# A graph attention and normalisation kernel: another order of work at the beginning, and the transpose of h moved into the step before

## The chip, the cores and the metric

The kernel runs on one core of a Trainium2 chip, with its five engines: TensorE (PE: matmuls and transposes), VectorE (DVE), ScalarE (ACT), GpSimd (POOL) and SyncE (SP, which issues every transfer here). The metric is the device time of one execution in microseconds; less is better. Inputs and outputs lie in the chip's main memory, and the clock runs from launch to the last store.

## The reference

There are 128 graphs of 64 nodes with 384 features, all in float32. Two graph layers stand between residual additions and normalisations:

```python
x = layernorm(x + L0(x, adj))            # eps 1e-5
x = layernorm(x + L1(x, adj))
# L0: masked attention, 12 heads of 32, per graph
q, k, v = x @ Wq + bq, x @ Wk + bk, x @ Wv + bv
s = where(adj > 0, q k^T / sqrt(32) + beta * adj, -9e15);  out = softmax(s) v
# L1: two layers, each with weights Wl, Ws, Wr of 384 x 384
a = softmax(h h^T / sqrt(384)) * adj;  attn = a / (sum(a) + 1e-10)
ctx = (attn above the diagonal) (h Wl^T + bl) + diag(attn) * (h Ws^T + bs) + (attn below it) (h Wr^T + br)
h = relu(layernorm(ctx, eps=1e-12) * g + b)
```

## The kernel before

**Units and stages.** A unit is 256 tokens: four graphs, held as T = 2 tiles of 128 tokens, each with two graphs. There are 32 units. The kernel is one software pipeline over steps s = -2 to 32. In step s four units are in work at once: `EARLY` (unit s+2: projections of q, k and v), `MID` (unit s+1: scores, softmax, attention output and the first residual normalisation, which leaves h0), `LATE` (unit s: the two layers of L1) and `FINAL` (unit s-1: the last normalisation and the store). Step -2 has only `EARLY` (called `begin` in the code), step -1 has `EARLY` and `MID` (`second`), step 0 is the first with `LATE`, step 30 has no `EARLY` any more and step 31 no `MID`.

**Split products.** Every float32 product with a weight is made of three matmuls: `product` (lines 304 to 306) multiplies hi by hi, hi by lo and lo by hi, where hi is the value in the rounded type fp32r and lo is the rest. So each weight (nine of them: V, Q, K and six of L1) is first split: ACT copies it to `w_hi` (L521 in three pieces for V, L529 for the others), DVE subtracts to get `w_lo` (L689, L695). x transposed (`xT_in`) is split in the same way by ACT (L536) and POOL (L990), and h transposed by ACT (`hT_hi`, L572) and DVE (`hT_lo`, L774). The raw weights land in three slots `w_raw` laid over the tile `late`, so a load of weight n >= 3 waits until the weight three before has been split.

**Order.** Nothing is scheduled by a tool: each engine has a function `step(st)` that issues its instructions in an order written by hand, and semaphores tie the engines together (`need` waits for a count that follows from the unit's number). Each engine works strictly in its own order. PE's order in a full step is:

- `transpose_h`: six 128x128 transposes of h0 (L398) into PSUM banks 4 and 5 (`HT_BANKS`);
- `scores` of `MID`: 96 small matmuls (L357) into banks 0 to 3;
- `gram(0)`: h times h transposed (L421, 24 matmuls) into bank 6, from `hT`, which ACT copies out of banks 4 and 5 (L570). It also waits until the sum of the unit before has left bank 6 (`ctx_ready`, DVE L837);
- `project_sides(0)`: four times nine matmuls with `hT_hi` and `hT_lo`, into banks 7, 4, 5 and 6; the first waits until the second half of the unit before has left bank 7 (`ctx_ready`, DVE L846);
- `transpose_e(0)` (L449), `project_self(0)` (twice nine matmuls), `mix(0)` (L467, 16 matmuls);
- `project_v`, `project_qk` parts 0 and 1, `transpose_z` (L408), `transpose_probs` (L372), `project_qk` part 2, `attend` (L387);
- `gram(1)`, `project_sides(1)`, `transpose_e(1)`, `project_self(1)`, `mix(1)` for the second layer.

The next step then begins with `transpose_h`. ACT in the end of a step normalises h0 (L617), scales the self term (L606, and in two halves L610), and in the next step splits x of `EARLY` (L536), then takes `hT` (L570) and `hT_hi` (L572).

**The beginning.** Step -2 loads x transposed, the weights V, Q, K and small columns in this order; PE then projects v of unit 0, then q and k of unit 0 in three parts m (18 matmuls each: nine for q, nine for k, 128 columns of the weight). V goes to banks 3 and 0, q and k to banks 1 and 2, where part 2 waits until part 1 has been read out (`QK_BANKS`). `take_qk` on ACT (L544, L546) moves them out. Step -1 has the scores of unit 0, v of unit 1 (which waits for `s_masked`, DVE L744, because its banks hold scores), the transposes of the probabilities, `attend`, and q and k of unit 1. V moves inside SBUF by four transfers (`v_halves`), issued by SP. The bias rows of L1 are one transfer of 1.5 MB (`vectors`).

Of the kernel before, what the change touches and what calls it, by code (L numbers as in the profile page):

```python
# [5 lines left out]
F32 = mybir.dt.float32  # L6
# [22 lines left out]
STAGES_BEFORE, STAGES_AFTER = 2, 1  # L29
NEG = 9000000000000000.0  # L30
# [60 lines left out]
def resnorm_kernel(nc, x, xT, adj, adjT, w, cols, beta, bv, vectors, out):  # L91
    ctx = ExitStack()
    with ctx:
# [39 lines left out]
        c = [c0, c1]  # L133
        RAW = 3
        w_raw = [late[:, r * KC * D:(r + 1) * KC * D].rearrange("p (k d) -> p k d", k=KC)
# [3 lines left out]
        columns = sb("columns", [P, 4, KC])  # L139
        bq_col, bk_col, g0_col, b0_col = (columns[:, i, :] for i in range(4))  # L140
        beta_col = sb("beta_col", [P, 1])
# [39 lines left out]
        wv_hi_set, wv_lo_set = sem("wv_hi_set"), sem("wv_lo_set")  # L181
        raw_in = [sem(f"raw_in{r}") for r in range(RAW)]
# [42 lines left out]

        block = ctx.enter_context(nc.Block())
# [3 lines left out]
        def _(sp):  # L230
# [5 lines left out]
            def load_x(st, ahead):  # L236
                slot = st.slot(ahead)
                need(sp, x_added, st.count(ahead - 2, 2, 2))
                sp.dma_start(x_in[:, slot], x[st.unit(ahead)]).then_inc(x_loaded[slot], 16)
                sp.dma_start(adj_in[:, slot], adj[st.unit(ahead)]).then_inc(adj_loaded[slot], 16)  # L240
                for g in range(GRAPHS):
                    half = slice(g * N, (g + 1) * N)
                    sp.dma_start(adjT_in[half, slot, :, half], adjT[st.unit(ahead), half]
                                 ).then_inc(adjT_loaded[slot], 16)

            def raw_weight(n):
                if n == RAW:
                    sp.wait_ge(wv_hi_set, KC)
                    sp.wait_ge(wv_lo_set, KC)
                if n > RAW:  # L250
                    sp.wait_ge(w_hi_set, n - RAW)
                    sp.wait_ge(w_lo_set, n - RAW)
# [4 lines left out]
            sp.dma_start(columns[:, :, :], cols).then_inc(cols_in, 16)  # L257
            sp.dma_start(beta_col[:, :], beta.partition_broadcast(P)).then_inc(cols_in, 16)
            raw_weight(1)
            raw_weight(2)  # L260
            sp.dma_start(bv_row, bv.partition_broadcast(P)).then_inc(bv_in, 16)
            sp.wait_ge(tiles_cleared, 4)

            def step(st):
                if st.unit(EARLY) == 0:
                    load_x(st, MID + 1)
                    for n in (3, 4, 5):
                        raw_weight(n)
                if st.unit(MID) == 0:
                    raw_weight(6)  # L270
                    raw_weight(7)
                if st.has(EARLY + 1):
                    load_xT(st, EARLY + 1)
                if st.has(MID + 1) and not st.unit(EARLY) == 0:
                    load_x(st, MID + 1)
                if st.unit(EARLY) == 0:
                    sp.dma_start(rows[:, 1:9, :].rearrange("p r d -> p (r d)"), vectors.partition_broadcast(P)
                                 ).then_inc(rows_in, 16)
                if st.unit(MID) == 0:
                    raw_weight(8)  # L280
# [3 lines left out]
                if st.has(EARLY):  # L284

                    need(sp, v_staged, st.count(EARLY, 2, 2))
                    need(sp, o_scaled, st.count(MID, 2, 2))
                    for g in range(GRAPHS):
                        for half in range(2):
                            src = v_stage[g * N:(g + 1) * N, :, half * PAIRS:(half + 1) * PAIRS, :]  # L290
# [798 lines left out]
```

## Time and profile before

| | before |
|---|---|
| median of 3 runs | 1321.81 us (1319.84 to 1321.83) |
| the profiled execution, its own time | 1321.77 us |
| span from first to last instruction | 1320.0 us |
| PE matmul busy | 1268.5 us (96%) |
| DVE busy | 997.4 us (76%) |
| ACT busy | 624.3 us (47%) |
| POOL busy | 369.0 us (28%) |
| chain that ended last | PE 95%, issue 1%, ACT 1%, DVE 1%, DMA 1% |

The profile is one execution. In its timeline a row is a start in us from the span's start, a duration, the engine, the line, what is written and read with the shapes, and a count; in square brackets stands the idle time of that engine before the row and the instruction whose end released it. Matmuls overlap, so the difference of two starts tells what a group costs PE, and a matmul's own duration does not. PEclk or "granted clock" is 1.00 where TensorE runs at 2.4 GHz and 0.50 at 1.2 GHz.

### The profile page before, as it was taken

The numbers are of one execution on the slowest core, as the hardware profiler recorded it, in microseconds if no ns is written. First come the engines' busy times: TensorE is split into PE (matmuls) and PEld (weight loads), VectorE is DVE, ScalarE is ACT, GpSimd is POOL, SyncE is SP. The second block draws the span as 40 slices with busy tenths as digits, with TensorE's granted clock in tenths as the row PEclk, the third lists the DMA queues.
The fourth block names the chain that finished last, engine by engine and source line by source line (L and its number), as shares of the span: only waits on it lengthen the run. The fifth ranks groups of instructions, "written<-read, shape, count | busy, mean of one in ns | idle before, by whom it ended". The sixth has DMA issues, their size and how long they took to land.

```text
span 1320.0 us, 34323 instructions
## 1 busy us (share of the span) xinstructions
PE 1268.5 (96%) x13824; PEld 1169.8 (89%) x13824; DVE 997.4 (76%) x2667; ACT 624.3 (47%) x1325; POOL 369.0 (28%) x399
## 2 busy tenths in 40 slices
PE   5999999999999999999999999999999999999885
PEld 5899999999999999999999999999999999999774
DVE  4658787778787778787778787778787778787765
ACT  4445445345445345545445545445544445544432
POOL 3213232223232223232223232323232323232211
PEclk9999999999999999999999999999999999999996
DMA  8111101111101111101111101111101111100000
GB/s 293 50 44 56 56 13 45 56 56 56 56 16 42 56 56 56 56 19 39 56 56 56 56 21 37 55 56 56 56 23 35 55 56 56 55 26 20 25 13 25
DMA packets 52206, 66.32 MB, mean 50 GB/s; under 512 B 17872, under 2 KB 38480, under 8 KB 51920
## 3 DMA queue, kind: packets, MB, share of 16 engines
q1 hardware_dynamic: 52048, 64.12, 16.0%
q8 instruction: 110, 1.80, 0.6%
q14 instruction: 48, 0.39, 0.1%
HBM read 38.54 MB, written 12.58 MB: 39 GB/s over the span
## 4 chain that ended last, share of the span: by engine, by line
PE 95%; issue 1%; ACT 1%; DVE 1%; DMA 1%; SPq 0%; POOL 0%; POOLq 0%; ACTq 0%; DVEq 0%
PE bank L304 24%; PE bank L306 23%; PE bank L305 23%; PE bank L467 7%; PE bank L421 4%; PE bank L387 4%; PE bank L372 3%; PE bank L357 3%; PE bank L398 2%; PE bank L408 2%; PE bank L449 1%; DMA late<-in_w 1%; DVE ln_six L856 0%; ACT late L623 0%; ACT w_hi L529 0%
## 5 line engine op out<-in xcount | busy, mean ns | idle before, releaser
L304 PE MATMUL bank<-w_hi,hT_hi 128*128 128x384 f32 x1152 | 399.9, 347 | 9.3 <-ACT hT_hi L572 8.4
L305 PE MATMUL bank<-w_lo,hT_hi 128*128 128x384 f32 x1152 | 388.7, 337 | 0.0
L306 PE MATMUL bank<-w_hi,hT_lo 128*128 128x384 f32 x1152 | 388.7, 337 | 0.0
L304 PEld LDWEIGHTS bank<-w_hi,hT_hi 128*128 128x128 f32 x1152 | 217.6, 189 | 15.0 <-ACT hT_hi L572 11.8
L305 PEld LDWEIGHTS bank<-w_lo,hT_hi 128*128 128x128 f32 x1152 | 218.1, 189 | 0.0
L306 PEld LDWEIGHTS bank<-w_hi,hT_lo 128*128 128x128 f32 x1152 | 217.6, 189 | 0.0
L810 DVE TENSOR_TENSOR hlr<-bank,rows 128x384 f32<-128x384 f32 x256 | 142.4, 556 | 88.7 <-PE bank L306 88.4
L1026 POOL TENSOR_TENSOR ln_rstd<-ln_var,minus_half 128x2 f32<-128x2 f32 x128 | 98.4, 769 | 352.1 <-DVE ln_var L862 132.6
L1013 POOL TENSOR_TENSOR probs<-probs,row_max 128x768 f32<-128x768 f32 x64 | 95.4, 1492 | 315.1 <-DVE row_max L750 315.1
L606 ACT ACTIVATE late<-late,diag 128x384 f32<-128x384 f32 x64 | 39.5, 617 | 276.2 <-DVE late L825 276.2
L304 PE MATMUL bank<-xT_hi,w_hi 128*128 128x256 f32 x576 | 163.9, 285 | 3.2 <-ACT kT L546 1.9
L305 PE MATMUL bank<-xT_lo,w_hi 128*128 128x256 f32 x576 | 161.1, 280 | 0.0
L306 PE MATMUL bank<-xT_hi,w_lo 128*128 128x256 f32 x576 | 160.9, 279 | 0.0
L825 DVE TENSOR_TENSOR late<-bank,rows 128x384 f32<-128x384 f32 x128 | 71.4, 558 | 104.5 <-PE bank L306 104.5
L990 POOL TENSOR_TENSOR xT_lo<-xT_in,xT_hi 128x768 fp32r<-128x768 f32 x32 | 59.4, 1855 | 211.6 <-ACT xT_hi L536 211.6
L304 PEld LDWEIGHTS bank<-xT_hi,w_hi 128*128 128x128 f32 x576 | 108.2, 188 | 4.0 <-issue 2.8
L306 PEld LDWEIGHTS bank<-xT_hi,w_lo 128*128 128x128 f32 x576 | 109.6, 190 | 0.0
L305 PEld LDWEIGHTS bank<-xT_lo,w_hi 128*128 128x128 f32 x576 | 108.2, 188 | 0.0
L610 ACT ACTIVATE late<-late,diag 64x384 f32<-64x384 f32 x128 | 78.5, 613 | 56.7 <-DVE late L825 55.0
L597 ACT ACTIVATE e_di<-bank,u_bias 128x128 f32<-128x128 f32 x128 | 45.8, 363 | 116.8 <-DVE u_bias L789 116.8
L467 PE MATMUL bank<-hlr,aT 64*64 64x386 f32 x1024 | 97.8, 497 | 0.0
L617 ACT ACTIVATE h<-h,ln_shift,ln_rstd 128x384 f32<-128x384 f32 x64 | 41.9, 702 | 98.1 <-DVE ln_shift L710 98.1
(89 smaller groups left out, 2336.7 us busy)
## 6 DMA issues: line engine op xcount, KB each, us to landing
v_halves<-v_stage SPq DMA_DIRECT2D x128, 99.0 KB, 2.3
xT_in<-in_xT SPq DMA_DIRECT2D x32, 384.0 KB, 3.4
x_in<-in_x SPq DMA_DIRECT2D x32, 384.0 KB, 3.9
out<-late SPq DMA_DIRECT2D x32, 384.0 KB, 2.4
late<-in_w SPq DMA_DIRECT2D x9, 576.0 KB, 7.0
adj_in<-in_adj SPq DMA_DIRECT2D x32, 96.0 KB, 3.7
adjT_in<-in_adjT SPq DMA_DIRECT2D x64, 48.0 KB, 3.2
rows<-in_vectors SPq DMA_DIRECT2D x1, 1536.0 KB, 10.5
```

Source lines behind the costliest of these rows:

```text
L304: nc.tensor.matmul(o, l_hi, r_hi, start=first and n == 0, stop=False)
L305: nc.tensor.matmul(o, l_hi, r_lo, start=False, stop=False)
L306: done = nc.tensor.matmul(o, l_lo, r_hi, start=False, stop=final and n == last)
L387: done = nc.tensor.matmul(o[g * N:(g + 1) * N, h:h + 3:2, :], pT[:, t * PAIRS + j, g * N:(g + 1) * N], v[:, :, j, :], start=True, stop=True)
L421: done = nc.tensor.matmul(U_BANK[g * N:(g + 1) * N, t * N:(t + 1) * N], a, a, start=kc == 0, stop=kc == KC - 1)
L467: done = nc.tensor.matmul(CTX_BANKS[t][o * N:(o + 1) * N, 0:MW], aT[rows_of, t, m, rows_of], hlr[rows_of, t, m, 0:MW], start=m == LEFT, st ...
L610: nc.scalar.activation(self_turned[o * N:(o + 1) * N], h_self[rows_of, 1], ACT.Copy, scale=diag[rows_of, 1:2]).then_inc(self_scaled, 1)
L810: nc.vector.tensor_tensor(hlr[:, t, m, 0:D], HLR_BANKS[2 * t + m][:, 0:D], bias_row[l][m], ALU.add).then_inc(hlr_ready, 1)
L825: nc.vector.tensor_tensor(h_self[:, t], SELF_BANKS[t][:, 0:D], bias_row[l][SELF], ALU.add).then_inc(self_ready, 1)
L990: nc.gpsimd.tensor_tensor(xT_lo[:, :, :], xT_in[:, slot], xT_hi[:, :, :].bitcast(F32), ALU.subtract).then_inc(xlo_ready, 1)
L1013: nc.gpsimd.tensor_tensor(s, s, row_max[:, t * H:(t + 1) * H].unsqueeze(2).to_broadcast([P, H, N]), ALU.subtract).then_inc(s_shifted, 1)
L1026: nc.gpsimd.tensor_tensor(rstd[:, :], var[:, :], minus_half[:, :], ALU.pow).then_inc(s_rstd, 1)
```

## The change

The change has these parts:

1. **Loads.** The raw weights Q and K come first, each in three column parts of 128 columns (six transfers of 192 KB, in runs of 512 bytes), each pair with a semaphore; V follows. `beta` is packed into `columns`, so its own transfer is gone. Bias rows, x and the other weights come in another order (`begin` and `second` of SP).
2. **First projections.** q and k of unit 0 part by part as their weight parts are split, then the scores; v of unit 0 only behind the scores. x of unit 0 is split into two tiles of its own (laid over `hT_hi` and `hT_lo`), and its low part is made by DVE, not POOL.
3. **Banks.** The first two units use banks that are free then: v in 4 and 5 or 6 and 7, q and k in 1, 2, 3 or 1, 2, 5, the probabilities in 3, 0, 4.
4. **Warm-up.** 20 transposes of the identity on PE before the first projection, as soon as the identity is made.
5. **h transposed sooner, in every step.** `transpose_h` is now issued in the step before, between the two halves of `project_self(1)`, into banks 1 and 2 (`H_BANKS`). ACT copies `hT` right behind normalising h0, then splits `hT_hi` from SBUF; DVE makes `hT_lo` at the end of its step. `scores` gets a wait for `hT` having left banks 1 and 2. ACT's scaling of the self term is cut in two functions, so that its second half (`scale_turned`, L610) now stands behind the split of `hT_hi`.

The diff, cut to its core:

```diff
+PREWARM = 20
...
+        x0_hi, x0_lo = (tile[:, :, :, :].rearrange("p t k i -> p (t k i)").rearrange("p (k n) -> p k n", k=KC)
+                        for tile in (hT_hi, hT_lo))
...
+        FIRST_V_BANKS = [[bank[4], bank[5]], [bank[6], bank[7]]]
+        FIRST_QK_BANKS = [[bank[1], bank[2], bank[3]], [bank[1], bank[2], bank[5]]]
+        FIRST_PT_BANKS = [bank[3], bank[0], bank[4]]
+        H_BANKS = [bank[1], bank[2]]
...
# SP
             def raw_weight(n):
-                if n == RAW:
+                if n in (3, 4):
+                    sp.wait_ge(wqk_hi_set, 2 * KC)
+                    sp.wait_ge(wqk_lo_set, 2 * KC)
+                elif n == 5:
                     sp.wait_ge(wv_hi_set, KC)
                     sp.wait_ge(wv_lo_set, KC)
...
             sp.dma_start(xT_in[:, 0], xT[0]).then_inc(xT_loaded[0], 16)
-            raw_weight(0)
...
+            for m in range(KC):
+                part = slice(m * P, (m + 1) * P)
+                for n in (W_Q, W_K):
+                    sp.dma_start(w_raw[RAW_OF[n]][:, :, part], w[n][:, :, part]).then_inc(qk_raw_in[m], 16)
+                if m == 0:
+                    sp.dma_start(columns[:, :], cols).then_inc(cols_in, 16)
+            sp.dma_start(w_raw[RAW_OF[W_V]], w[W_V]).then_inc(raw_in[RAW_OF[W_V]], 16)
...
+            def begin(st):
+                load_adj(0)
+                load_xT(st, EARLY + 1)
+                sp.dma_start(bv_row, bv.partition_broadcast(P)).then_inc(bv_in, 16)
+                raw_weight(3)
+                raw_weight(4)
+                sp.dma_start(x_in[:, 0], x[0]).then_inc(x_loaded[0], 16)
+                raw_weight(5)
+
+            def second(st):
+                load_adj(1)
+                sp.dma_start(x_in[:, 1], x[1]).then_inc(x_loaded[1], 16)
+                move_v(st, MID)
+                sp.dma_start(rows[:, 1:9, :].rearrange("p r d -> p (r d)"), vectors.partition_broadcast(P)
+                             ).then_inc(rows_in, 16)
+                raw_weight(6)
+                raw_weight(7)
+                load_xT(st, EARLY + 1)
+                raw_weight(8)
+                move_v(st, EARLY)
...
# PE
             def scores(st):
                 need(pe, qk_ready, st.count(MID, 6, 6))
...
+                need(pe, hT_ready, st.count(LATE, 5, 2))
...
             def transpose_h(st):
...
+                if st.has(EARLY):
+                    need(pe, qk_ready, st.count(EARLY, 6, 6))
+                need(pe, pT_ready, st.count(MID, 3, 3))
+                for t in range(T):
+                    need(pe, h0_ready, st.count(MID, 2, t + 1))
                     for kc in range(KC):
...
+                        done = nc.tensor.transpose(H_BANKS[t][:, kc * P:(kc + 1) * P],
+                                                   h0[:, st.slot(MID), t, kc * P:(kc + 1) * P], ident[:, :])
...
+            pe.wait_ge(mask_steps, 2)
+            for n in range(PREWARM):
+                nc.tensor.transpose(bank[7][:, 0:P], ident[:, :], ident[:, :])
             pe.wait_ge(consts_set, 1)
+
+            def begin(st):
+                for m in range(3):
+                    project_qk(st, m)
+
+            def second(st):
+                scores(st)
+                project_v(st, MID)
+                project_qk(st, 0)
+                transpose_probs(st)
+                project_qk(st, 1)
+                attend(st)
+                project_qk(st, 2)
+                project_v(st, EARLY)
+                transpose_h(st)
...
                     transpose_e(st, 1)
-                    project_self(st, 1)
+                    project_self(st, 1, 0)
+                if mid:
+                    transpose_h(st)
+                if late:
+                    project_self(st, 1, 1)
                     mix(st, 1)
...
# ACT
+            def begin(st):
+                split_x(st)
+                split_qk_weights()
+                scale_bq()
+                take_qk(st, 0)
+                split_v_weight()
+                take_qk(st, 1)
+                take_qk(st, 2)
+
+            def second(st):
+                split_x(st)
+                split_weight(3)
+                split_weight(4)
+                exp_scores(st, 0)
+                exp_scores(st, 1)
+                take_pT(st)
+                take_qk(st, 0)
+                split_weight(5)
+                take_qk(st, 1)
+                split_weight(6)
+                take_qk(st, 2)
+                normalize_h(st)
+                take_hT(st)
+                split_hT(st)
+                split_weight(7)
+                split_weight(8)
...
                 if mid:
...
+                    normalize_h(st)
+                    take_hT(st)
                 if late:
                     scale_self(st, 1)
+                if mid:
+                    split_hT(st)
+                if late:
+                    scale_turned(st, 1)
...
# DVE
+            def begin(st):
+                split_x0()
+                split_qk_weights()
+                split_v_weight()
+                make_add(st)
+
+            def second(st):
+                mask_scores(st, 0, 4)
+                max_scores(st, 0)
+                max_scores(st, 1)
+                stage_v(st, MID)
+                split_weight(3)
+                split_weight(4)
+                make_add(st)
+                heads_out(st)
+                split_weight(5)
+                stats_outer(st)
+                shift(st, MID, ln0_mv, ln0_rstd, ln0_shift, ln0_rs, ln0_sh)
+                stage_v(st, EARLY)
+                hT_low(st)
+                split_weight(6)
+                split_weight(7)
...
                     mask_aT(st, 0)
+                    if st.unit(LATE) == 0:
+                        split_weight(8)
                     self_bias(st, 0)
...
                     self_bias(st, 1)
+                if mid:
+                    hT_low(st)
```

Here `move_v` holds the four `v_halves` transfers, `load_adj` the adjacency loads, and `split_qk_weights` the split of the six parts.

## Rows read from the trace of the kernel before

**Rows 1.** Windows: length; PE, PEld, DVE, ACT, POOL busy; clock; DMA share; GB/s.
```profile
85.79:125.30 39.51, 39.23 (x434) 36.23 (x434) 30.75 (x83) 19.11 (x42) 11.38 (x12) 1.00 0.16 47
```

**Rows 2.** Timeline of PE around the end of one step.
```profile
594.51 0.42 PE L304 MATMUL bank<-w_hi,hT_hi 128*128 128x384 f32 x1
...
597.82 1.53 PE L467 MATMUL bank<-hlr,aT 64*64 64x386 f32 x16
...
599.27 0.88 PE L398 MATMUL bank<-ident,h 128*128 128x128 f32 x6
...
600.08 1.25 PE L357 MATMUL bank<-kT,qT 32*64 32x64 f32 x96
...
601.26 0.92 PE L421 MATMUL bank<-hT 128*64 128x64 f32 x24
...
602.47 0.41 PE L304 MATMUL bank<-w_hi,hT_hi 128*128 128x384 f32 x1 [0.28 <-ACT hT_hi L572]
```

**Rows 3.** Timeline of PE in the middle of the same step.
```profile
581.65 0.82 PE L408 MATMUL bank<-ident,late 128*128 128x128 f32 x6
...
582.30 1.47 PE L372 MATMUL bank<-ident,probs 128*128 128x128 f32 x12
...
587.22 0.87 PE L421 MATMUL bank<-hT 128*64 128x64 f32 x24
...
588.02 0.45 PE L304 MATMUL bank<-w_hi,hT_hi 128*128 128x384 f32 x1
```

**Rows 4.** Timeline of ACT around the same end of a step.
```profile
594.37 1.31 ACT L617 ACTIVATE h<-h,ln_shift,ln_rstd 128x384 f32<-128x384 f32 x2 [3.14 <-DVE ln_shift L710]
...
598.52 1.25 ACT L610 ACTIVATE late<-late,diag 64x384 f32<-64x384 f32 x2 [0.86 <-DVE late L825]
...
600.54 0.85 ACT L570 ACTIVATE hT<-bank 128x384 f32<-128x384 f32 x2
```

**Rows 5.** Timeline of DVE around the same end of a step.
```profile
597.92 0.56 DVE L825 TENSOR_TENSOR late<-bank,rows 128x384 f32<-128x384 f32 x1 [1.00 <-PE bank L306]
...
599.48 0.16 DVE L834 TENSOR_TENSOR den<-bank,dz 128x1 f32<-128x1 f32 x1 [0.99 <-PE bank L467]
...
600.51 0.56 DVE L846 TENSOR_TENSOR late<-bank,late 128x384 f32<-128x384 f32 x1
```

**Rows 6.** Timeline of PE in the first 49 us.
```profile
7.46 0.66 PE L304 MATMUL bank<-w_hi,xT_hi 128*128 128x384 f32 x1 [7.46 <-DVE w_lo L689]
...
22.96 1.25 PE L357 MATMUL bank<-kT,qT 32*64 32x64 f32 x96 [0.93 <-ACT kT L546]
...
26.35 0.66 PE L304 MATMUL bank<-w_hi,xT_hi 128*128 128x384 f32 x1 [2.13 <-DVE probs L744]
...
44.65 1.14 PE L398 MATMUL bank<-ident,h 128*128 128x128 f32 x6 [1.52 <-ACT h L617]
...
48.89 0.69 PE L304 MATMUL bank<-w_hi,hT_hi 128*128 128x384 f32 x1
```

**Rows 7.** Windows of the beginning, same columns.
```profile
14.38:18.46 4.08, 4.08 (x36) 4.08 (x36) 1.70 (x2) 2.86 (x4) 0.00 (x0) 1.00 0.97 355
...
7.46:12.80 5.34, 5.34 (x18) 5.33 (x18) 2.15 (x3) 2.49 (x3) 0.00 (x0) 1.00 1.00 355
```

**Rows 8.** Timeline of SP and ACT in the first 33 us.
```profile
2.65 0.91 SPq L253 DMA_DIRECT2D late<-in_w  x2
...
31.33 0.84 ACT L551 ACTIVATE probs<-probs 128x768 f32<-128x768 f32 x1 [1.70 <-POOL probs L1013]
```

**Rows 9.** DMA issues, KB each, median us from issue to landing.
```profile
late<-in_w SPq DMA_DIRECT2D x9, 576.0 KB, 7.0
...
rows<-in_vectors SPq DMA_DIRECT2D x1, 1536.0 KB, 10.5
```

**Rows 10.** Timeline of PE in step 30, and its window behind (same columns as rows 1).
```profile
1252.35 2.73 PE L372 MATMUL bank<-ident,probs 128*128 128x128 f32 x12
...
1255.00:1256.00 1.00, 1.00 (x33) 0.99 (x34) 0.60 (x4) 0.89 (x2) 0.28 (x1) 1.00 0.00 0
```

More of the change, by code:

```diff
@@ L181, in resnorm_kernel @@
         wv_hi_set, wv_lo_set = sem("wv_hi_set"), sem("wv_lo_set")
+        qk_raw_in = [sem(f"qk_raw_in{m}") for m in range(KC)]
+        wqk_hi_set, wqk_lo_set = sem("wqk_hi_set"), sem("wqk_lo_set")
         raw_in = [sem(f"raw_in{r}") for r in range(RAW)]
@@ L264, in step @@
             def step(st):
                 if st.unit(EARLY) == 0:
-                    load_x(st, MID + 1)
-                    for n in (3, 4, 5):
-                        raw_weight(n)
+                    begin(st)
+                    return
                 if st.unit(MID) == 0:
-                    raw_weight(6)
-                    raw_weight(7)
+                    second(st)
+                    return
                 if st.has(EARLY + 1):
                     load_xT(st, EARLY + 1)
-                if st.has(MID + 1) and not st.unit(EARLY) == 0:
+                if st.has(MID + 1):
@@ L284, in step @@
                 if st.has(EARLY):
[L286 to L290, printed above, removed]
-                            dst = v_halves[half * N:(half + 1) * N, :, g, half * PAIRS * VW:(half + 1) * PAIRS * VW]
-                            sp.dma_start(dst, src.rearrange("p t h d -> p t (h d)")).then_inc(v_moved, 16)
+                    move_v(st, EARLY)
             steps(step)
@@ L320, in project_v @@
                     for kc in range(KC):
[L321 removed]
+                        if unit == 0 and t == 0:
                             pe.wait_ge(wv_hi_set, kc + 1)
                             pe.wait_ge(wv_lo_set, kc + 1)
[L324 removed]
+                        done = product(v_banks(unit)[t][:, 0:D], [((hi[:, kc, tok], lo[:, kc, tok]), weight(W_V, kc))],
                                        first=kc == 0, final=kc == KC - 1)
@@ L361, in transpose_probs @@
             def transpose_probs(st):
-                if st.has(EARLY):
+                unit = st.unit(MID)
+                if unit == 0:
+                    need(pe, s_masked, st.count(MID, 4, 4))
+                    need(pe, v_staged, st.count(MID, 2, 1))
+                elif st.has(EARLY):
                     need(pe, v_staged, st.count(EARLY, 2, 2))
-                    if not st.unit(MID) == 0:
-                        need(pe, qk_ready, st.count(EARLY, 6, 2))
+                    need(pe, qk_ready, st.count(EARLY, 6, 2))
                 for t in range(T):
@@ L415, in gram @@
                 need(pe, ctx_ready[1 - l], st.count(LATE - 1 + l, 2, 1))
+                if l == 0 and st.unit(LATE) == 0:
+                    need(pe, v_staged, st.count(MID, 2, 2))
                 for t in range(T):
@@ L451, in transpose_e, with project_self @@
                 done.then_inc(eT_psum, 1)
-            def project_self(st, l):
-                for t in range(T):
-                    need(pe, hlr_ready, st.count(LATE, 8, 4 * l + 2 + t))
-                    project_h(st, l, t, SELF, SELF_BANKS[t]).then_inc(self_psum, 1)
+            def project_self(st, l, t):
+                if st.unit(LATE) == 0 and t == 0:
+                    pe.wait_ge(w_hi_set, 3 + 3 * l)
+                    pe.wait_ge(w_lo_set, 3 + 3 * l)
+                need(pe, hlr_ready, st.count(LATE, 8, 4 * l + 2 + t))
+                project_h(st, l, t, SELF, SELF_BANKS[t]).then_inc(self_psum, 1)
             def mix(st, l):
@@ L661, in step @@
                     take_zT(st)
-                if mid and not second:
+                if mid:
                     take_pT(st)
@@ L938, in step @@
                     shift(st, FINAL, ln2_mv, ln2_rstd, ln2_shift, ln2_rs, ln2_sh)
-                if mid and not second:
+                if mid:
                     heads_out(st)
@@ L1029, in step @@
                 late, mid, early, final = st.has(LATE), st.has(MID), st.has(EARLY), st.has(FINAL)
-                if early:
+                if early and not st.unit(EARLY) == 0:
                     split_x(st)
```

289 lines of the change are left out of this document (151 added, 138 removed).

## The prediction

> **What bounds the kernel now.** I read the busy time by window first: in one full step PE is busy 39.23 of 39.51 us at full clock, DVE 30.75, ACT 19.11, POOL 11.38 [rows 1]. So only PE's own instructions and PE's gaps make time, and the question for each edit is what it takes out of PE's row of instructions. The timeline of PE shows one gap in a full step: the first matmul of `project_sides(0)` starts 1.21 us behind the first of `gram(0)` and its row ends an idle time of 0.28 us released by ACT's `hT_hi` [rows 2]. Behind `gram(1)`, where the split is long done, the same stretch takes 0.80 us (587.22 to 588.02) [rows 3]. The other place where PE stands is the beginning: first matmul at 7.46 us, scores of unit 0 at 22.96, then waits of 2.13 us for the masked scores and 1.52 us for h0, and the first sides of step 0 only at 48.89 [rows 6]. The last two steps also have gaps, between the layers of L1; the change does not touch them. About 0.2% (2.6 us) is what a measurement of this kernel can tell from no change.
>
> **The full steps.** Count from the start of `mix(1)`. Before: mix 1.45 us, six transposes of h 0.81, scores 1.18, gram and its gap 1.21; together 4.65 us from 597.82 to 602.47 [rows 2]. After: the gap goes because hT and both splits are made a step's end earlier, so gram costs 0.80, as gram(1) does [rows 3]. The transposes are not saved but moved between two groups of nine 128-row matmuls. Six transposes between 128-row instructions took 0.65 us (581.65 to 582.30) [rows 3]; behind the 64-row mix they take 0.81 [rows 2]. The trace has no scores directly behind a mix; the bounds of that switch are nothing and the same 0.16. So after is 1.45 + 1.18 + 0.80 plus 0.65 to 0.81 plus 0 to 0.16: 4.08 to 4.40 us, a gain of 0.25 to 0.57 per step. I take 0.42, near the middle, since neither end has a row of the same neighbours.
>
> The steps from 0 to 30 have 30 such step ends with scores behind them: 12.6 us. Into step 31 there are no scores to cover DVE's sum of the unit before, so gram would then wait for that instead of hT: I count 0.1. Sum **12.7** (range 7.6 to 17.2).
>
> That needs four new orders to hold, each checked against the same step.
> - *Transposes wait for h0.* ACT ends normalising h0 at 595.68 [rows 4]. The first half of `project_self(1)` ends 9 of the 18 matmuls behind 594.51, at 596.16 [rows 2]. Slack 0.5 us.
> - *Scores wait for hT out of banks 1 and 2.* ACT needs 0.85 us [rows 4], from about 596.6; PE needs it behind nine matmuls and a mix, at 599.9. Slack over 2 us.
> - *ACT's `scale_turned` (1.25 us, at 598.52 before [rows 4]) now stands behind hT, h_self and hT_hi.* The second hT_hi waits for `project_self(1)` to end, moved to about 598.5, so it starts near 599.2, 0.7 us later. DVE's last sum (L846, from 600.51 [rows 5], 2.69 us behind the mix's start) would be wanted at 601.17; ACT is done at 600.4.
> - *DVE has two `hT_low` (two of the kind of 0.5 us) ahead of the sum of the unit before.* Its self bias ends at about 599.1, the two at 600.1, and its first wait for the mix ends 1.66 us behind the mix's start [rows 2, 5], which would be 600.14. The last sum then ends 3.25 us behind the mix's start, and the sides want bank 7 at 3.43. This is the tightest: 0.2 us.
> In the body of the step DVE's scores, POOL's and ACT's work come some tenths sooner; they hide behind PE as before. The order of SP's transfers in full steps is unchanged.
>
> **The beginning.** I follow PE's clock until the first sides of step 0 (48.89 before).
> *First data.* Before, x and a 576 KB weight had to land; now x and two parts of 192 KB, a fifth fewer bytes, but in runs of 512 bytes, of which the trace has no load. Bounds for the first matmul: 6.5 us (bytes count), 9.1 (the parts at half the rate); I take 7.1, nearer to the row 7.46 [rows 6].
> *q and k of unit 0.* 36 matmuls took 4.08 us [rows 7], so 54 take 6.1. SP issues one load in 0.46 us [rows 8], so the last part is issued near 4 us and lands, with the 7.0 us median of the weights [rows 9], at 11; with its split and the last 18 matmuls (2.0) that is 14.4; PE alone would be done at 13.2. I take 14.0. ACT has V's split ahead of `take_qk(1)`, so the scores start 1.2 us later, at 15.2 instead of 22.96.
> *Warm clock.* At half clock 12 transposes took 2.73 us [rows 10]; 20 take 4.5, from about 1.6 us on (estimates): they end by 6 us, ahead of the first data, and cost nothing. If they lift the clock they save what V paid: 5.34 us for 18 matmuls [rows 7] against 3.3 for 18 in the full step [rows 2], 2.0 us. Step 30 shows that it can be so: those 12 ran at 0.23 us each, twice the 0.11 of rows 3, so at 1.2 GHz, and at their end, from 1255.00 on, the granted clock is 1.00 [rows 10].
> *Behind the scores.* v of unit 0 (3.1 us) fills what was the 2.13 us wait, to 19.5. q, k part 0: to 21.6. The probabilities: before, the second exponential ended 9.2 us behind the scores' start (32.17 against 22.96) [rows 6, 8]; so PE transposes the second half at 24.4, with the first half done, a stand of some 1.7 us: to 24.8. Part 1: to 26.9. `attend` needs v moved: staged at 21.3, four issues, 2.6 us, landing 2.5 us later, near 26.5: no wait. To 28.4. Part 2 (2.1) and v of unit 1 (3.1): to 33.6. h0 of unit 0: in the full step it was done 8.5 us behind `attend` (587.22 to 595.68) [rows 3, 4]; here fewer foreign operations stand in between, so 6.5: at 35.0; a new stand of about 1 us takes the place of the 1.52. Transposes, the copy of hT (0.85) as a new exposed wait, scores, gram and the low split: sides at 39.2.
> So the beginning gives 48.89 - 39.2 = **9.7 us**. The moved loads: the 1.5 MB of bias rows is issued at 24 us instead of 15 and lands 10.5 us later at most [rows 9], 34.5, before DVE wants it near 41. Weight 6 lands behind it, near 32; ACT splits it ahead of `take_qk(2)`, which must be out before the transposes of h. That is the one load that can reach PE. In step 0 DVE still has splits 7 and 8 among its work, and sides' biases come late: I charge 0.5 us.
>
> **Sum.** 9.7 + 12.7 - 0.5 = 21.9 us. Against the profiled run's 1321.77 (span 1320.0), which is the median 1321.81 within 0.1, that is 1299.9.
>
> One rule speaks against the warm-up. The Trainium skill, page "TensorE: Matmul & The Clock Gate", Part 4, says that the full clock does not engage for PE transposes. By it the first projections would run at half clock and the sum be 2.0 us smaller, 1301.9. Rows 10 say otherwise.
>
> **The rivals.**
> - *The beginning gives only half* (chance 0.17). Place: short runs of the weight parts, or weight 6 behind the bias rows: if that lands at 36 instead of 32, `take_qk(2)`, the transposes and all behind are 3 to 4 us late. Gain 5 + 12.7: 1304.
> - *The cold start* (0.08): the transposes do not lift the clock, because the rise at 1255 had another cause than they. 1302.
> - *The gap only changes its name* (0.12). The sides wait for bank 7 (slack 0.2 us) instead of hT_hi: if DVE's two `hT_low` start 0.5 us later than I think, because hT_hi comes late from ACT, the last sum is 0.3 to 0.4 late and the full steps give nearly nothing. For it: four engines' orders meet there. Gain 9.7 to 11: 1311.
> - *Slower* (0.04). The transposes of h now stand in the middle of `project_self(1)`, and h0 has 0.5 us of slack where it had 3.6. If the chain POOL, DVE, ACT in front of it comes later than before by x, every step pays x - 0.5. With the gains above it decides at x = 0.5 + 0.7 = 1.2 us; at 1.5 us 30 steps cost 30, less 21.9: 1330. Against it: nothing in that chain was moved later.
> - The change not doing what it says would be scores stalled by its new wait for banks 1 and 2; it has 2 us of slack and is in the cases above.
>
> **The numbers.** Forecast case 0.59, 1299.9, itself 1294 to 1306. The range takes in the half beginning, the cold start and the upper bounds of the gain: 1293 to 1308, which leaves out the renamed gap, the slower case and a small part above. Faster by over 0.2%: 0.94; within: 0.02; slower: 0.04.
>
> **What would show it.** Right: first matmuls of q and k near 7 us at full clock (starts 0.11 us apart); scores of unit 0 near 15; sides of step 0 near 39; in full steps gram to sides 0.80 us with no idle time, a period of 39.1 instead of 39.5; L398 rows with no idle time. Wrong: an idle time before the sides released by DVE's sum of the unit before, one before the transposes of h released by ACT's h, or a period of 39.5 or more.

## The result, and the profile after

The changed kernel took 1300.70 us (median of 4, 1299.78 to 1301.35), the kernel before 1321.82 in the same rounds: a ratio of 0.9842 with a 95% interval of 0.9825 to 0.9859. The forecast was 1299.9 us with a range of 1293 to 1308. The profiled execution took 1300.28 us and has a span of 1298.6, so 21.4 us less span than before. One execution of the kernel before, in the rounds of experiments 5, 9 and 10, took 3945.57 us; it is left out of the comparisons.

In the numbers of lines 304 to 306 are now 354 to 356, scores L422, the transposes of h L469, gram L495, mix L543, the warm-up L551. The busy row of the page, then the windows of one full step and of the stretch with the slow clock (columns as in rows 1):

```profile
PE 1263.3 (97%) x13844; PEld 1169.9 (90%) x13844; DVE 1009.4 (78%) x2672; ACT 629.9 (49%) x1329; POOL 368.0 (28%) x398
```

```profile
85.00:124.03 39.03, 39.03 (x434) 36.20 (x433) 31.20 (x84) 19.28 (x41) 11.40 (x12) 1.00 0.17 48
...
34.00:46.00 12.00, 9.40 (x148) 8.77 (x149) 8.00 (x14) 7.98 (x16) 3.48 (x4) 0.72 0.54 166
```

A full step is PE alone now: 39.03 us of matmuls in 39.03 us, where [rows 1] have 39.23 in 39.51.

The timeline of PE around the end of a step, which answers to [rows 2]:

```profile
582.83 0.34 PE L356 MATMUL bank<-w_hi,hT_lo 128*128 128x384 f32 x1
583.01 0.82 PE L469 MATMUL bank<-ident,h 128*128 128x128 f32 x6
...
584.19 0.33 PE L354 MATMUL bank<-w_hi,hT_hi 128*128 128x384 f32 x1
...
585.32 1.53 PE L543 MATMUL bank<-hlr,aT 64*64 64x386 f32 x16
586.78 1.25 PE L422 MATMUL bank<-kT,qT 32*64 32x64 f32 x96
587.96 0.92 PE L495 MATMUL bank<-hT 128*64 128x64 f32 x24
588.81 0.44 PE L354 MATMUL bank<-w_hi,hT_hi 128*128 128x384 f32 x1
```

From mix to the first sides it is 3.49 us instead of 4.65. The idle 0.28 is gone. The transposes stand inside `project_self(1)`: from the product at 582.83 to the fourth behind it at 584.19 it is 1.36 us, where four products alone take 0.70 (0.174 from start to start), so they cost 0.66. Together 4.15 against 4.65.

DVE's rows of the same place show how little there is left to spare ([rows 5]):

```profile
585.90 1.02 DVE L922 TENSOR_TENSOR hT_lo<-hT,hT_hi 128x384 fp32r<-128x384 f32 x2
...
588.00 0.56 DVE L994 TENSOR_TENSOR late<-bank,late 128x384 f32<-128x384 f32 x1
```

The sum that frees bank 7 ends at 588.56, 0.25 us before the sides want the bank.

The timeline of PE in the first 41 us, which answers to [rows 6]:

```profile
1.59 4.53 PE L551 MATMUL bank<-ident 128*128 128x128 f32 x20 [1.59 <-POOL ident L1134]
7.46 0.36 PE L354 MATMUL bank<-hT_hi,w_hi 128*128 128x256 f32 x1 [1.34 <-DVE w_lo L830]
...
14.98 1.27 PE L422 MATMUL bank<-kT,qT 32*64 32x64 f32 x96 [0.93 <-ACT kT L654]
...
21.96 0.85 PE L441 MATMUL bank<-ident,probs 128*128 128x128 f32 x6 [0.27 <-ACT probs L659]
...
26.22 1.62 PE L456 MATMUL bank<-v_halves,pT 128*64 128x66 f32 x48
...
35.97 1.05 PE L469 MATMUL bank<-ident,h 128*128 128x128 f32 x6 [2.75 <-ACT h L729]
37.65 1.77 PE L422 MATMUL bank<-kT,qT 32*64 32x64 f32 x96 [0.63 <-issue]
39.35 1.55 PE L495 MATMUL bank<-hT 128*64 128x64 f32 x24
40.83 0.69 PE L354 MATMUL bank<-w_hi,hT_hi 128*128 128x384 f32 x1
```

The first product comes at 7.46, later than the 7.1 of the forecast; from the scores to `attend` all is a little ahead of it (scores 14.98 against 15.2, the second six transposes of the probabilities 23.29 against 24.4, attend 26.22 against 26.5). Then PE stands 2.75 us for h0, and what follows runs slowly: scores 1.70 us from start to start instead of 1.18, gram 1.48 instead of 0.85. ACT's timeline says why h0 is late:

```profile
33.34 1.16 ACT L633 ACTIVATE w_hi<-late 128x1152 fp32r<-128x1152 f32 x1 [5.98 <-DMA late<-in_w]
34.41 0.46 ACT L652 ACTIVATE qT<-bank,columns 128x256 f32<-128x256 f32 x1
...
35.12 1.30 ACT L729 ACTIVATE h<-h,ln_shift,ln_rstd 128x384 f32<-128x384 f32 x2
```

ACT has stood 5.98 us for weight 6 (`w_hi` of L633), with `take_qk(2)` and the normalisation of h0 queued behind. That load is issued at 24.54, behind the 1.5 MB of bias rows at 23.84, as SP's timeline shows:

```profile
23.84 0.60 SPq L319 DMA_DIRECT2D rows<-in_vectors  x1
24.54 0.88 SPq L284 DMA_DIRECT2D late<-in_w  x2
```

**Where the 21.4 us came from**, by the first sides of each step in both traces. Up to those of step 0: 48.89 - 40.83 = 8.06 us. From there to step 1: 40.02 before, 40.40 after, -0.38. The 29 steps to step 30: 88.91 to 1234.17 before, 81.23 to 1213.23 after, 13.26 or 0.457 per step. Step 30 to 31: 37.01 and 37.41, -0.40. From step 31's sides to the end: 48.82 and 47.96, 0.86. These are the two profiled executions, one each.

### The profile page after: what moved, and what is told of

Same layout as the page of the kernel before. It is cut to its first block, busy times and chain, and to the rows that moved or that the text cites. A ratio compares the mean times of both kernels' runs of the same rounds, so it can differ in the third digit from the quotient of the medians.

```text
span 1298.6 us, 34540 instructions
## 1 busy us (share of the span) xinstructions
PE 1263.3 (97%) x13844; PEld 1169.9 (90%) x13844; DVE 1009.4 (78%) x2672; ACT 629.9 (49%) x1329; POOL 368.0 (28%) x398
## 4 chain that ended last, share of the span: by engine, by line
PE 95%; DVE 2%; DMA 1%; issue 1%; ACT 1%; SPq 0%; POOL 0%; POOLq 0%; ACTq 0%; DVEq 0%
PE bank L354 24%; PE bank L356 23%; PE bank L355 23%; PE bank L543 7%; PE bank L495 4%; PE bank L456 4%; PE bank L441 3%; PE bank L422 3%; PE bank L479 2%; PE bank L469 2%; PE bank L523 1%; DMA late<-in_w 1%; DVE ln_six L1004 0%; ACT late L735 0%; SPq L294 0%
## 5 line engine op out<-in xcount | busy, mean ns | idle before, releaser
L354 PE MATMUL bank<-w_hi,hT_hi 128*128 128x384 f32 x1158 | 405.1, 350 | 1.0 <-issue 0.8
L354 PE MATMUL bank<-xT_hi,w_hi 128*128 128x256 f32 x558 | 158.7, 284 | 0.0
L355 PE MATMUL bank<-xT_lo,w_hi 128*128 128x256 f32 x558 | 156.1, 280 | 0.0
L356 PE MATMUL bank<-xT_hi,w_lo 128*128 128x256 f32 x558 | 155.9, 279 | 0.0
L356 PEld LDWEIGHTS bank<-xT_hi,w_lo 128*128 128x128 f32 x558 | 106.2, 190 | 0.0
L355 PEld LDWEIGHTS bank<-xT_lo,w_hi 128*128 128x128 f32 x558 | 104.9, 188 | 0.0
L354 PEld LDWEIGHTS bank<-xT_hi,w_hi 128*128 128x128 f32 x558 | 104.8, 188 | 0.1
L543 PE MATMUL bank<-hlr,aT 64*64 64x386 f32 x1024 | 97.8, 497 | 0.0
```

Source lines behind the costliest of these rows:

```text
L354: nc.tensor.matmul(o, l_hi, r_hi, start=first and n == 0, stop=False)
L355: nc.tensor.matmul(o, l_hi, r_lo, start=False, stop=False)
L356: done = nc.tensor.matmul(o, l_lo, r_hi, start=False, stop=final and n == last)
L543: done = nc.tensor.matmul(CTX_BANKS[t][o * N:(o + 1) * N, 0:MW], aT[rows_of, t, m, rows_of], hlr[rows_of, t, m, 0:MW], start=m == LEFT, st ...
```

## The experiments

All were run beside the kernel before, whose medians lay between 1321.8 and 1322.1. An experiment has four or five executions, which lie within 1.0 to 3.9 us of each other. The unchanged changed kernel was run once more as `e12_again`: 1300.67 us (1299.99 to 1301.57).

**1. h sooner, alone** (part 5 put into the kernel before, nothing else).

```diff
 # PE, kernel before (ACT's and DVE's part as in the change)
-                if late:
-                    transpose_h(st)
...
+                    project_self(st, 1, 0)
+                if mid:
+                    transpose_h(st)
+                if late:
+                    project_self(st, 1, 1)
```

> The kernel before with part 5 alone: h transposed in the step before, in every step, the beginning as it was. Theory: 0.48 us less per full step, 30 times 0.48 and something at the first, 13 to 15 us in all: 1307 to 1309 against 1321.8. Rival (the gap only changes its name): under 3 us.

1309.24 us (1307.64 to 1310.74), 12.6 less than before, at a ratio of 0.9907 (0.9891 to 0.9924), with a period of 39.04. So part 5 gives 12.6, and 8.5 of the 21.1 are left for the other four. These were not run without part 5, so that the two add up is no result of its own; but the 8.5 fit the 8.06 that the traces show up to the first sides of step 0, and the forecast's 12.7 and 9.2 (9.7 - 0.5). The waits of PE in this kernel (us in total, times, longest) have no row any more for `hT_hi`; the five longest:

```profile
PE bank L410 <- ACT late L631: 11.1, 2, 5.5
PE bank L305 <- DVE w_lo L702: 7.5, 1, 7.5
PE bank L305 <- DVE probs L757: 2.1, 1, 2.1
PE bank L305 <- ACT kT L550: 2.0, 2, 1.0
PE bank L400 <- ACT h L625: 1.6, 1, 1.6
```

**2. The place of the transposes** (in front of both halves of `project_self(1)` instead of between them).

```diff
+                if mid:
+                    transpose_h(st)
                 if late:
                     project_self(st, 1, 0)
-                if mid:
-                    transpose_h(st)
-                if late:
                     project_self(st, 1, 1)
```

> The changed kernel, with the transposes of h in front of both halves of project_self(1) instead of between them, 1.65 us sooner on PE. By the trace h0 is then 0.5 us (first tile) and 1.15 us (second) late, and PE stands 0.9 us per step: 27 us more, near 1327, slower than the kernel before. Rival (h0 does come sooner when PE asks for it, or the stand is caught up later in the step): under 5 us more.

1327.33 us, slower than before (1.0046, 1.0031 to 1.0061). PE's timeline:

```profile
593.14 1.06 PE L469 MATMUL bank<-ident,h 128*128 128x128 f32 x6 [0.46 <-ACT h L729]
593.96 0.42 PE L354 MATMUL bank<-w_hi,hT_hi 128*128 128x384 f32 x1
```

From `transpose_e` to the mix it takes 4.96 us where the changed kernel takes 4.10; 0.86 for 31 steps is 26.7 us, the 26.6 that the median rose. The wait itself is only 0.46 of it; 0.25 more is the time from the transposes' start to the next product (0.82 instead of 0.57); the rest was not taken apart. This is what the slower rival describes, made to happen: nine matmuls of cover ahead of the transposes decide between 21 us gained and 5 lost.

**3. DVE's slack** (one more addition of 128x384 behind `hT_low`, in steps 1 on).

```diff
                 if mid:
                     hT_low(st)
+                    if late and st.unit(LATE) >= 1:
+                        nc.vector.tensor_tensor(spare[:, :], rows[:, 1, :], rows[:, 2, :], ALU.add)
```

> The changed kernel with one more DVE addition of 128x384 (0.47 us) behind hT_low in each step from 1 on (its result is not used). Theory: the last sum of the unit before has 0.25 us of slack before project_sides(0), so each of some 30 steps gets 0.2 to 0.25 us longer: 6 to 8 us more, 1307 to 1309, with idle time of PE before the sides or before gram. Rival (slack is larger, or nothing waits there): under 2 us more.

1305.54 us (1305.03 to 1307.96), 4.8 more: less than expected. PE's and DVE's timelines:

```profile
589.96 0.92 PE L496 MATMUL bank<-hT 128*64 128x64 f32 x24
591.02 0.41 PE L355 MATMUL bank<-w_hi,hT_hi 128*128 128x384 f32 x1
```

```profile
588.82 0.55 DVE L1122 TENSOR_TENSOR spare<-rows 128x384 f32<-128x384 f32 x1
...
590.31 0.56 DVE L995 TENSOR_TENSOR late<-bank,late 128x384 f32<-128x384 f32 x1
```

The added 0.47 us make the last sum end at 590.87 and the sides start at 591.02: gram to sides takes 1.06 instead of 0.85, and the period is 39.225 instead of 39.034. 0.47 put in, 0.2 paid: the slack is what is in between, about 0.25. It lies in two places. DVE's first sum behind the mix begins 1.99 us behind the mix's start instead of 1.66, so 0.14 of the 0.47 goes into a wait that DVE had there; the last sum ends 0.33 later (3.57 against 3.24), and the sides start 0.23 later, 0.15 behind its end. So of the 0.25 between that end and the sides in the changed kernel only 0.10 was to spare. Past the slack every step pays. 29 periods of 0.19 more are 5.55 us, and the span rose by 5.0: up to the first sides of step 0 this execution is 1.17 longer, step 0 is 1.34 shorter, step 30 is 0.17 longer and the end 0.55 shorter.

**4. No warm-up** (`PREWARM = 20` to 0).

> The changed kernel without its 20 warm-up transposes. If they lift the clock: the first 18 matmuls of q and k (256 columns) start about 0.21 us apart instead of 0.118 until the clock rises, and 1.5 to 2.5 us are lost at the beginning (near 1303 against 1300.7). If transposes don't lift it, or the clock is up anyway: starts stay 0.118 us apart, no difference.

1301.15 us (1300.93 to 1301.97), 0.5 more. PE's timeline:

```profile
7.66 0.55 PE L354 MATMUL bank<-hT_hi,w_hi 128*128 128x256 f32 x1 [7.66 <-DVE w_lo L830]
8.00 0.42 PE L355 MATMUL bank<-hT_lo,w_hi 128*128 128x256 f32 x1
...
17.19 1.25 PE L422 MATMUL bank<-kT,qT 32*64 32x64 f32 x96 [0.93 <-ACT kT L654]
```

Products start 0.21 us apart until 12.28, against 0.118 with the warm-up, so they run at 1.2 GHz, and the scores come 2.2 us later. Less of it arrives at the end. The first sides come at 43.13, 2.3 later, yet at full clock, where the changed kernel's first nine still go at half rate; those of step 30 are 1.3 later, those of step 31 0.8, and the span is 1.6 longer, by clock steps in the last two steps that differ. The medians are 0.5 us apart, less than the executions of one kernel differ among themselves, so the worth of the warm-up in the whole is not told from nothing here; the 1.5 to 2.5 us expected are not there.

**5. 30 warm-up transposes instead of 20.**

> The changed kernel with 30 warm-up transposes instead of 20, so that they end near 7.0 to 7.5 us, where the first product can start. Theory (the stand behind the warm-up lets the clock fall in some executions): products at full clock in every execution, scores near 15.0, the median 0 to 1.5 us lower than with 20. Rival (the clock's fall has nothing to do with the stand): the same as with 20; if the transposes run at half clock all the time they end at 8.4 and cost 1 us.

1299.83 us (1299.66 to 1301.25) beside 1300.67 for the repeat: not told apart. PE's stand before the first product is 0.73 us instead of 1.34, and the scores come at 14.85. PE's timeline of the warm-up, the whole of it and then a stretch near its end:

```profile
1.59 5.22 PE L551 MATMUL bank<-ident 128*128 128x128 f32 x30 [1.59 <-POOL ident L1134]
...
5.66 1.04 PE L551 MATMUL bank<-ident 128*128 128x128 f32 x8
```

In the changed kernel 20 take 4.53 us, 0.22 from start to start. Here the last eight take 1.04; the last of them lasts 0.27, so they start 0.11 apart. PE had run nothing but transposes until then: they alone have brought it to full rate.

**6. Weights Q and K whole** instead of in three column parts.

```diff
-            for m in range(KC):
-                part = slice(m * P, (m + 1) * P)
-                for n in (W_Q, W_K):
-                    sp.dma_start(w_raw[RAW_OF[n]][:, :, part], w[n][:, :, part]).then_inc(qk_raw_in[m], 16)
+            for n in (W_Q, W_K):
+                sp.dma_start(w_raw[RAW_OF[n]], w[n]).then_inc(qk_raw_in[0], 16)
...
-                    act.wait_ge(qk_raw_in[m], 32)
+                    act.wait_ge(qk_raw_in[0], 32)
...
-                    dve.wait_ge(qk_raw_in[m], 32)
+                    dve.wait_ge(qk_raw_in[0], 32)
```

> The changed kernel, with Q and K loaded whole (576 KB each, runs of 4.6 KB) instead of by column parts; splits and projections stay by parts. If the parts matter: the first k waits for all of K, the scores of unit 0 start 1.5 to 3 us later than 15.0, 1 to 3 us more in all. Rival (runs of 512 bytes cost what the parts give): scores near 15, no difference.

1301.97 us (1300.51 to 1302.38), 1.3 more, with ranges that overlap, so the total is not told apart. The first product starts at 8.46 instead of 7.46, the scores at 17.38. One microsecond is the parts' own; the other 1.4 us is the clock, which fell just behind the start in this execution (products 0.21 apart from 8.9 to 12.1), as it also did in others whose weights came in parts.

**7. Part 2 of q and k of unit 0 back in bank 2**, behind the read-out of part 1.

```diff
-        FIRST_QK_BANKS = [[bank[1], bank[2], bank[3]],
+        FIRST_QK_BANKS = [[bank[1], bank[2], bank[2]],
...
-                if m == 2 and unit >= 2:
+                if m == 2 and unit != 1:
                     need(pe, qk_ready, st.count(EARLY, 6, 4))
```

> The changed kernel, with part 2 of q and k of unit 0 in bank 2 again (it waits for part 1 to be read out) instead of a bank of its own. ACT reads part 1 out behind V's split, at 13.8 us, so part 2 starts 2 us later than 11.7, the scores near 17. The total: 2 us more if the beginning is one chain; under 1 us if the landing of weight 6 at 33 us absorbs it.

1303.19 us (1302.44 to 1306.36), 2.5 more. PE's timeline:

```profile
14.43 0.55 PE L354 MATMUL bank<-hT_hi,w_hi 128*128 128x256 f32 x1 [2.88 <-issue]
```

PE stands 2.88 us and starts again at half clock; the scores come at 19.54, 4.6 later. About half of it is left in the medians.

**8. Weight 6 off the path, two ways.** Split it on ACT behind h0's work:

```diff
                 take_qk(st, 1)
-                split_weight(6)
                 take_qk(st, 2)
                 normalize_h(st)
                 take_hT(st)
                 split_hT(st)
+                split_weight(6)
```

> The changed kernel, with ACT's split of weight 6 moved behind take_qk(2), the normalisation of h and the two copies of hT. Theory: the landing of weight 6 at 33.3 us holds take_qk(2), and with it the transposes of h. Then the transposes start near 34.1 us (behind DVE's shift at 33.25) instead of 35.97: 1.9 us less, and up to 2.8 us more if the shorter stand keeps the clock up: 1296 to 1299 against 1300.7. Rival: h0 itself is late (GpSimd's slower additions), then the transposes stay near 36 us and nothing is gained.

or load it ahead of the bias rows, with a wait of its own ahead of DVE's first use of those:

```diff
-                sp.dma_start(rows[:, 1:9, :] ...).then_inc(rows_in, 16)
                 raw_weight(6)
                 raw_weight(7)
+                sp.dma_start(rows[:, 1:9, :] ...).then_inc(rows_in, 16)
...
             def sides_bias(st, l, t, m):
+                if st.unit(LATE) == 0 and (l, t, m) == (0, 0, LEFT):
+                    dve.wait_ge(rows_in, 16)
```

> The changed kernel, with weights 6 and 7 loaded ahead of the 1.5 MB of bias rows (and a wait for these rows ahead of their first use, which the other order of loads made needless). ACT's order stays. If it was the landing of weight 6 that held take_qk(2), this gives the same as splitting it later: ACT's split of weight 6 no more at 33.3 us but before 31, the transposes of h near 34 to 35, 2 to 3 us less (1298 to 1299). Price that may appear: the rows land later, 35 to 40 us; DVE wants them near 45. If it gives nothing, the later split gained by ACT's freed time, not by the load.

1298.14 (1297.33 to 1299.47) and 1298.07 us (1296.34 to 1299.07), both 2.6 less than the changed kernel. The transposes of h in the first and in the second:

```profile
35.07 1.05 PE L469 MATMUL bank<-ident,h 128*128 128x128 f32 x6 [0.92 <-ACT h L729]
```

```profile
29.14 1.17 ACT L633 ACTIVATE w_hi<-late 128x1152 fp32r<-128x1152 f32 x1 [0.53 <-DMA late<-in_w]
...
35.42 1.06 PE L469 MATMUL bank<-ident,h 128*128 128x128 f32 x6 [0.95 <-ACT h L729]
```

They start 7.9 us behind the start of `attend` in both, against 9.75 in the changed kernel, and two edits that share nothing but weight 6 give the same. So that load was on the path, for 1.8 us plus the clock that PE lost while it stood. What holds the transposes now is h0 itself: they start 6.4 us behind the end of `attend`, for which the forecast had 6.5.

**9. The ends too.** Experiment 8's first order, and 44 transposes of the identity on PE ahead of `transpose_z` in steps 30 and 31, where PE stands 5.5 us and then runs at half clock.

```diff
+                if late and not early:
+                    if mid:
+                        need(pe, s_masked, st.count(MID, 4, 4))
+                    need(pe, self_ready, st.count(LATE, 4, 2))
+                    for n in range(GAP_WARM):
+                        nc.tensor.transpose(bank[2][:, 0:P], ident[:, :], ident[:, :])
                 if late:
                     transpose_z(st)
```

> The changed kernel with the split of weight 6 behind the copies of hT, and 44 transposes of the identity into a free bank in the stands of steps 30 and 31 ahead of transpose_z (PE waits 5.5 us there, and then runs at half clock). They take 4.8 us of 5.5 at full clock. Theory: 12+6 transposes and attend of step 30 and the second layer of step 31 run at full clock: 2 us and 3 us less; with the 2.6 us of the later split 1293 to 1295. Rival: the work behind these stands waits for ACT and DVE anyway: 1298.

1296.36 us (1294.01 to 1297.40), a ratio of 0.9803 (0.9790 to 0.9816), the lowest median here, 4.3 below the changed kernel and 1.8 below experiment 8's order alone. Its profiled execution is the lowest of its five, 1294.01. Step 30 in the changed kernel and then in this one:

```profile
1230.09 1.51 PE L479 MATMUL bank<-ident,late 128*128 128x128 f32 x6 [5.55 <-ACT late L735]
1231.40 2.77 PE L441 MATMUL bank<-ident,probs 128*128 128x128 f32 x12
...
1236.01 0.86 PE L495 MATMUL bank<-hT 128*64 128x64 f32 x24
```

```profile
1220.85 5.02 PE L596 MATMUL bank<-ident 128*128 128x128 f32 x44
1226.47 0.85 PE L480 MATMUL bank<-ident,late 128*128 128x128 f32 x6 [0.60 <-ACT late L742]
1227.16 1.47 PE L442 MATMUL bank<-ident,probs 128*128 128x128 f32 x12
1229.80 1.63 PE L457 MATMUL bank<-v_halves,pT 128*64 128x66 f32 x48 [1.17 <-ACT pT L672]
1231.24 0.89 PE L496 MATMUL bank<-hT 128*64 128x64 f32 x24
```

From `transpose_z` to gram(1) it is 4.77 us instead of 5.92. The transposes fall to 0.69 and 1.47, half of 1.31 and 2.70; 1.17 of what that gives goes into a new wait, for ACT's copy of the transposed probabilities. `transpose_z` itself is not later: 7.08 us behind the start of the mix ahead of it, 7.07 in the changed kernel. From the scores of step 30 to the end of the span the two kernels take 87.40 and 84.74 us, 2.7 less; 1.1 of it in step 30 and 1.6 behind it, where 2 and 3 were expected (the second sides of step 31 to `transpose_e` take 6.31 instead of 7.92). The other part of this execution's gain is a beginning with weight 6 off the path and no fall of the clock (first sides of step 0 at 37.73).

**10. All of it together** (experiment 8's second order, 30 transposes at the start, 44 at the ends, and 6 and 5 around the transposes of h in step -1).

> All together: weights 6 and 7 loaded ahead of the bias rows, 30 warm-up transposes, 6 and 5 transposes around transpose_h of step -1 (stands of 0.9 and 0.6 us), and 44 in the stands of steps 30 and 31. 2.6 + 1 + 1 + 5 us less than the changed kernel: 1291 to 1293.

1297.48 us (1295.35 to 1299.12), 4 us above what was expected and not told apart from experiment 9. The transposes of h come at 34.19 as hoped, gram at 37.08; then PE's timeline has

```profile
39.96 0.41 PE L355 MATMUL bank<-w_hi,hT_hi 128*128 128x384 f32 x1 [1.97 <-DVE w_lo L855]
```

an idle time of 1.97 us that no other kernel here has. DVE's L855 ends there, but it splits weights 6 and 7, and the sides of step 0 wait for weights 3 and 4 only, long split. So the releaser is only the nearest event, and the cause of this stand stays open.

## Why the forecast held, point by point

- **Full steps: 0.42 forecast, 0.46 to 0.50 measured.** At one end it is 4.65 - 3.49 - 0.66 = 0.50, over 29 steps 0.457 each. The unknown was the switch from mix to scores, taken between nothing and 0.16: it costs nothing (1.46 from start to start, as before the switch to transposes). Gram came out at 0.85, not 0.80, and the moved transposes at 0.66, the low end of 0.65 to 0.81. The gain per period is some 0.04 below that of the end, and 0.03 of it stands in the sides behind: without an idle time ahead of them they take 6.35 us to `transpose_e`, with it 6.32 (the step that starts at 562.97 before, at 549.78 after).
- **The four orders held.** h0 0.5 us ahead of its transposes (ACT ends 582.52, PE wants it at 583.01), the last sum 3.24 us behind the mix's start (3.25 forecast), 0.25 between the sum and the sides (0.2 forecast). Experiments 2 and 3 show that both margins are real: used up, the first turned the result, and 0.47 us of work against the second took 5 us of it.
- **The beginning: 9.7 forecast, 8.06 measured.** This is the term that was too large. The chain was right up to the end of v of unit 1 (33.06, forecast 33.6). "at 35.0; a new stand of about 1 us" failed: the transposes of h came at 35.97 behind 2.75 us, since weight 6 landed at 33.3 (forecast "near 32") with `take_qk(2)` and the normalisation behind it. The forecast names this load as the one that can reach PE, and prices it as a rival; it came in between. The step that was mis-sized is this wait: 2.75 us where 1 was forecast. And from there to the sides 4.86 us passed instead of 4.2, because PE had stood and its clock fell: in experiment 9, where it did not fall, the same stretch took 3.77 (33.96 to 37.73). The forecast put a fall of the clock there at nothing without a reason; it cost 1.1 us, of which 0.4 were hidden in a stretch taken too long. The 0.97 of the first and the 0.66 of the second make the 1.64.
- **The warm-up: 2.0 forecast, 2.2 at the scores, 0.5 in the medians, which is not told from nothing.** The mechanism was right and its worth was not: later stands and clock steps take most of it.
- **Step 0 and the last steps.** For step 0 the forecast had 0.42 of gain less 0.5, so -0.08; -0.38 was measured. The 0.5 were charged for DVE's splits, and these never reach PE: from the end of the first sides on step 0 has no idle time of PE and the lengths of a full step. What was lost is clock: those sides take 7.72 us instead of 6.84, since nine products instead of three go at half rate, 0.88 against 0.50 gained. So this term was near for a wrong reason. The 0.1 of gain into step 31 became -0.40: in step 30 the stretch from the probabilities' transposes to gram(1) took 4.61 us instead of 4.16, the clock rising later. Step 31 gave 0.86 that nobody forecast, also by the clock (the second sides to `transpose_e`: 7.92 us against 9.14). So the terms miss by -1.64 (beginning), -0.30 (step 0), +1.08 (29 steps at 0.457 instead of 0.42), -0.50 and +0.86 (the end), and the sum by -0.50: it is closer than its parts, by luck.
- **The half beginning** (0.17) has its mechanism confirmed at a third of its size; **the gap renamed** and **slower** did not happen by 0.25 and 0.5 us.

## What to carry to other kernels

Once an engine has no gap left in the steady step, look at what it runs between different shapes and where the next engine's last work ends: here the 0.5 us by which h0 is ahead decided over 27 us (experiment 2), and 0.47 us of work against DVE's 0.25 took 5 (experiment 3), so measure the slack by adding a little work before building on it. A load whose consumer sits in order ahead of critical work should be issued ahead of larger ones that are needed later, or its consumer moved back; both cost nothing here and gave 2.6 us. At the beginning a microsecond won early was worth about half or less at the end, since stands and the clock take the rest (0.5 of 2.2 us, 1.3 of 2.4 and 2.5 of 4.6 in experiments 4, 6 and 7, of which only the last is clear of what executions differ by).

## What the runs showed of the hardware

- **Transposes do lift TensorE's clock.** Without the 20 float32 transposes the first products start 0.21 us apart, with them 0.118 (experiment 4), and in experiment 5 the transposes themselves go from 0.22 to 0.11 us apart before anything else has run. The Trainium skill, page "TensorE: Matmul & The Clock Gate", Part 4, says that the full clock does not engage for PE transposes; for these transposes the runs say otherwise. They also hold it: in experiment 9 44 of them fill a stand, 5.02 us in all, 0.11 apart, and the rows behind run at full rate.
- **What the clock does behind a short stand varies from run to run.** Behind the warm-up PE stands 0.7 to 2.6 us (not at all in experiment 10). In the profiled executions of the changed kernel and its repeat the first products run at full rate throughout; in experiments 3, 6 and 8 (second) the rate halved within about a microsecond and came back 3 to 4 us later, and in experiment 8 (first) it was halved from the start until 10.3. One profile of each kernel does not tell how often.
- **The granted clock is not on record from the start.** Windows from 9 to 11 us of experiment 8 (second) and of experiment 4, in both of which products start 0.21 us apart there (columns as in rows 1):

```profile
9.00:11.00 2.00, 2.00 (x11) 2.00 (x11) 1.26 (x3) 1.01 (x4) 0.00 (x0) 0.50 0.99 313
```

```profile
9.00:11.00 2.00, 2.00 (x12) 2.00 (x11) 1.30 (x3) 1.03 (x3) 0.00 (x0) 1.00 1.04 328
```

  Where the rate fell behind the start (experiments 3, 6 and 8, second) the column shows it. Where products were at half rate from the first on (experiments 4 and 8, first, and the kernel before, whose first 18 products take 5.34 us at a column of 1.00 in [rows 7]) it reads 1.00. So in the first microseconds a 1.00 does not mean 2.4 GHz, and the distance of the starts tells the rate.
- **A small shape after another can be free.** Scores behind mix cost nothing (1.46 us from the mix's start to theirs, 1.18 for the scores themselves, as with the transposes in between). The six transposes between mix and scores took 0.81 us to the next group, those between products and other transposes 0.65 ([rows 2, 3]); which of the two neighbours costs the 0.16 is not shown.
